# The self term of a graph layer's output: from a multiply-add on VectorE to a diagonal product on TensorE

## The reference

```python
def _gat_layer(x, src, dst, W, a_src, a_dst, b, heads, d_out, concat):
    h = (x @ W).reshape(N, heads, d_out)
    ...
    alpha = ex / (denom[dst] + 1e-16)
    msg = alpha[:, :, None] * h[src]
    out = jax.ops.segment_sum(msg, dst, num_segments=N)
    ...
loops = jnp.arange(N)
src = jnp.concatenate([edge_index[0], loops])
dst = jnp.concatenate([edge_index[1], loops])
...
x = x + gnn(_layernorm(x), ...)
x = x + ffn(_layernorm(x)[None], ...)[0]     # 768 -> 96 -> gelu -> 768
```

## Time and profile before

| | |
|---|---|
| median of three runs | 4394.83 us (4390.88 to 4399.89) |
| profiled execution | 4393.57 us, span 4391.8 us, mean granted clock of TensorE 0.911 |
| TensorE busy | 3519.7 us, 80% of the span |
| TensorE weight loads | 2144.6 us, 49% |
| VectorE busy | 2160.0 us, 49% |
| ScalarE, GpSimd | 30%, 25% |

### The profile page before, as it was taken

How to read it: one execution, slowest core, us unless ns; L and a number is a source line. 1 busy time by engine, 2 the same in 40 slices (tenths; PEclk the granted TensorE clock), 3 DMA queues, 4 the chain that set the end, 5 groups by cost and what they waited for, 6 DMA issues and landing times. The chain is left out here.

```text
span 4391.8 us, 67315 instructions
## 1 busy us (share of the span) xinstructions
PE 3519.7 (80%) x21804; PEld 2144.6 (49%) x21805; DVE 2160.0 (49%) x5207; ACT 1302.9 (30%) x2233; POOL 1088.3 (25%) x1396
## 2 busy tenths in 40 slices
PE   4850018999999999999999999999999900078988
PEld 3640005665556655565556655665556500055665
DVE  8877135334433444344433444344434200289998
ACT  3531104223332333223322333233322200034444
POOL 2447731000000000000000000000000067466665
PEclk9975559999999999999999999999999955589999
DMA  8862001111111111111111111111111000178887
GB/s 257 256 194 60 3 16 49 52 38 49 41 45 52 40 42 42 56 37 46 38 52 37 52 40 43 53 38 43 43 55 39 24 6 1 28 208 230 235 230 207
DMA packets 147719, 338.13 MB, mean 77 GB/s; under 512 B 81378, under 2 KB 82178, under 8 KB 140030
## 3 DMA queue, kind: packets, MB, share of 16 engines
q1 hardware_dynamic: 112047, 240.87, 18.1%
q0 software_dynamic: 34240, 93.39, 8.9%
q10 hardware_dynamic: 1175, 0.05, 0.0%
HBM read 266.08 MB, written 124.25 MB: 89 GB/s over the span
## 5 line engine op out<-in xcount | busy, mean ns | idle before, releaser
L934 POOL DMA_INDIRECT lay_rows<-parts,lay_idx x200 | 210.1, 1051 | 2533.1 <-PE lay_pz L1177 1615.8
L1211 PE MATMUL lay_pm<-lay_zh,w1h 128*128 128x500 f16 x1920 | 717.6, 374 | 26.5 <-DVE lay_h L1097 21.2
L1212 PE MATMUL lay_pm<-lay_zl,w1h 128*128 128x500 f16 x1920 | 717.9, 374 | 2.1 <-issue 1.7
L1213 PE MATMUL lay_pm<-lay_zh,w1l 128*128 128x500 f16 x1920 | 717.8, 374 | 0.0
L1018 DVE SCALAR_TENSOR_TENSOR lay_zl<-lay_pz,lay_zh 128x400 f16<-128x400 f32 x600 | 319.6, 574 | 708.5 <-ACT lay_zh L1128 708.5
L1128 ACT ACTIVATE lay_zh<-lay_pz 128x400 f16<-128x400 f32 x600 | 298.3, 504 | 1054.7 <-PE lay_pz L1177 1050.9
L1137 ACT ACTIVATE lay_ex<-lay_pm,b1c,scale 128x500 f32<-128x500 f32 x320 | 245.6, 768 | 869.5 <-PE lay_pm L1213 869.5
L1235 PE MATMUL lay_pm<-w2h,lay_gh 128*128 128x512 f16 x1280 | 484.9, 379 | 0.0
L1235 PE MATMUL lay_pm<-w2h,lay_gl 128*128 128x512 f16 x1280 | 483.9, 378 | 0.0
L1235 PE MATMUL lay_pm<-w2l,lay_gh 128*128 128x512 f16 x1280 | 483.4, 378 | 0.0
L1053 DVE TENSOR_SCALAR lay_ex<-lay_ex,scale 128x500 f32<-128x500 f32 x320 | 153.7, 480 | 568.2 <-ACT lay_ex L1137 568.2
(11 more groups left out here) (275 smaller groups left out, 5860.0 us busy)
## 6 DMA issues: line engine op xcount, KB each, us to landing
x<-in_x_dram SPq DMA_DIRECT2D x20, 1500.0 KB, 6.7
out_x<-x SPq DMA_DIRECT2D x100, 288.0 KB
out_own<-h SPq DMA_DIRECT2D x100, 288.0 KB
out_dram<-out_x SPq DMA_DIRECT2D x100, 288.0 KB
nrm_xb<-in_x_dram SPq DMA_DIRECT2D x20, 1344.0 KB
parts<-nrm_parts SPq DMA_DIRECT2D x20, 1344.0 KB
h<-lay_h SPq DMA_DIRECT2D x80, 336.0 KB
nrm_w<-in_L_gnn_W_dram SPq DMA_DIRECT2D x6, 1024.0 KB, 19.3
```

Source lines behind the costliest of these rows:

```text
L1211: pe.matmul(o, c.w1h[:, d, cols], zh[:, d, h], start=(d == 0), stop=False)
L1212: pe.matmul(o, c.w1h[:, d, cols], zl[:, d, h], start=False, stop=False)
L1213: ins = pe.matmul(o, c.w1l[:, d, cols], zh[:, d, h], start=False, stop=(d == DC - 1))
```

## The change

The self term moves from VectorE to TensorE. VectorE now writes for each tile a 100x100 diagonal matrix, `self_att`, the identity times the column of own weights, in the place where L1649 stood; it no longer reads `own` or `x` there. TensorE multiplies this diagonal by `own` and accumulates the product with that of `att` and `rows` in `pa`, in both column parts. The semaphore `own_added` is replaced: TensorE waits for `self_ready` and for the load of `own`, L1627 waits for the load of `x`, and SyncE frees a buffer of `own` by `agg_done`.

```diff
@@ stage_output, tiles
-        att = m.sb("att", [OE, AB, OT])
+        att, self_att = m.sb("att", [OE, AB, OT]), m.sb("self_att", [OT, AB, OT])
@@ SyncE, load_rows
-                    sp.wait_ge(own_added, t + 1 - HB)
+                    sp.wait_ge(agg_done, t + 1 - HB)
@@ VectorE, weights
-                    dve.wait_ge(own_added, GT * grp)
+                    dve.wait_ge(self_ready, GT * grp)
@@ VectorE, iteration
                     dve.wait_ge(agg_done, t + 1)
-                    dve.wait_ge(own_added, t + 1)
+                    dve.wait_ge(x_in[at], 32 * (grp + 1))
                     nc.vector.tensor_tensor(x[:, at], x[:, at], pa[0:OT, 0:D], ALU.add).then_inc(x2_ready, 1)
@@
                     spread(t2, at2)
-                    dve.wait_ge(x_in[at2], 32 * (there2 + 1))
-                    dve.wait_ge(own_in[at2 % HB], 32 * (2 * there2 + at2 // HB + 1))
-                    nc.vector.scalar_tensor_tensor(out=x[:, at2], in0=own[:, at2 % HB], scalar=w_own[:, at2:at2 + 1],
-                                                   in1=x[:, at2], op0=ALU.mult, op1=ALU.add).then_inc(own_added, 1)
+                    nc.vector.tensor_scalar(self_att[:, at2 % AB], c.ident[0:OT, 0:OT], w_own[:, at2:at2 + 1], None, ALU.mult)\
+                        .then_inc(self_ready, 1)
@@ TensorE, iteration
                     pe.wait_ge(gathered[at], 16 * (there + 1))
-                    pe.matmul(pa[0:OT, 0:512], att[:, at % AB], rows[:, at, 0:512], start=True, stop=True)
-                    pe.matmul(pa[0:OT, 512:D], att[:, at % AB], rows[:, at, 512:D], start=True, stop=True)\
-                        .then_inc(agg_done, 1)
+                    pe.wait_ge(self_ready, t + 1)
+                    pe.wait_ge(own_in[at % HB], 32 * (2 * there + at // HB + 1))
+                    for cols in (slice(0, 512), slice(512, D)):
+                        pe.matmul(pa[0:OT, cols], self_att[:, at % AB], own[:, at % HB, cols], start=True, stop=False)
+                        ins = pe.matmul(pa[0:OT, cols], att[:, at % AB], rows[:, at, cols], start=False, stop=True)
+                    ins.then_inc(agg_done, 1)
```

More of the change, by code:

```diff
@@ L1400, in stage_output @@
                 "turned", "xt_ready", "h_done", "u_ready", "t_ready", "th_ready", "g_ready", "o_done", "o_ready",
-                "own_added", "chain", "setup", "gelu", "prep", "bias_in", "held", "paused")
+                "self_ready", "chain", "setup", "gelu", "prep", "bias_in", "held", "paused")
         (par_in, turned_w, w_ready, init, posed, slots_in, idx_ready, mask_ready, looked, weights_ready,
          att_ready, agg_done, x2_ready, ve_ready, norm_ready, newton, xn_ready, turned, xt_ready, h_done, u_ready, t_ready,
-         th_ready, g_ready, o_done, o_ready, own_added, chain, setup, gelu, prep, bias_in, held, paused) = (
+         th_ready, g_ready, o_done, o_ready, self_ready, chain, setup, gelu, prep, bias_in, held, paused) = (
              m.sem(n) for n in sems)
```

## The result

The changed kernel takes 4429.77 us in the median of four runs (4427.81 to 4431.70), the one before 4392.87 in the runs beside it. The ratio is 1.0081 with a 95% interval of 1.0064 to 1.0099: 0.8% slower, as forecast. The profiled execution took 4428.32 us around a span of 4426.6.

The account below looks back on a forecast made before the run. VectorE bounds the kernel before, TensorE the changed one at 5.43 us per tile. Pace +32.1 and start +2.65 and +1.3 make +36 on 4393.6, about 4430 us; own range 4414 to 4445, stated range 4413 to 4452.

Parts of the forecast that it names:

- The bound and the room: In the loop, VectorE full at 4.79 us per tile, TensorE at 4.14, with 0.95 us of room there.
- The price of the product: TensorE's added 512- and 256-column f32 products take 1.29 us per tile, as the old aggregation and the projection do.
- The pace: Loop turns on TensorE of 5.43 us, 6.3 with look-ups; from tile 4 to tile 99, +32.1 us.
- The start: At tile 4: +2.65 us for its doubled aggregation, +1.3 for the transposes and first layer behind it.
- at the half clock: Tile 4's aggregation runs at 1.2 GHz, 2.65 us before the change, and doubles with the added product.
- The end of the span: Behind the last L1627 nothing changes: 19.7 us.
- VectorE's side at nothing: VectorE's tile loses 0.93 us (L1649), gains 0.27 (diagonal), to 4.13; this changes nothing if TensorE is the bound.
- The waits that go: In the loop, waits for gathered rows nearly gone, 10.3 us for own rows gone; lead grows 2 to 3 us.
- Rival A: TensorE has room: one record per product adds 0.645 us per tile, VectorE's relief counts, 4365 us; chance 0.04.
- B: Gathers stay late: a 1.0 us wait per group, then half clock, some 4 us per group, 4466 us; chance 0.11.
- C: TensorE's weight loads for the added products do not hide: 0.7 us per tile, 4496 us; chance 0.04.
- D: TensorE's added time comes near the room, 0.95 us per tile instead of 1.29: 4390 to 4400 us; chance 0.03.

## Why the prediction was right

**The bound and the room.** "VectorE full at 4.79, TensorE at 4.14 and 0.95 us of room per tile" was read from starts in the earlier trace rows. The run with the product on 512 columns, 0.86 us, comes out even; the changed kernel, 1.29, does not. That is the decisive step, and it is shown, though 0.95 itself is only bracketed by the two, and as a mean over the group it does not say what a single turn has: 0.65 in a plain one.

**The price of the product.** 1.29 us was taken from two neighbours of other heights. The trace after has 2.59 - 1.29 = 1.30, and the product issued twice adds it again.

**The pace.** 5.43 us per plain turn and 6.31 with look-ups were forecast as 5.43 and 6.3. From tile 4 to tile 99 the trace has 4406.65 - 3873.16 = 533.5 us against 531.9 computed; what is over are short delays before tile 5 of five groups (turns of 5.48 to 6.11), of which the trace names one as a wait for gathered rows.

**The start** was mis-sized: +3.95 us were reckoned and 3873.16 - 3872.28 = +0.9 came. The step that failed is "at the half clock" for tile 4: its aggregation took 2.64 us at full clock instead of 5.3 at half. The windows view from 3860 to 3870 us, of the kernel before, of the changed one, and of the one with both engines at work:

```profile
3860.00:3870.00 10.00, 5.32 (x23) 4.07 (x24) 5.90 (x18) 3.20 (x6) 7.34 (x17) 0.72 1.01 256
3860.00:3870.00 10.00, 4.77 (x31) 3.15 (x29) 6.34 (x23) 3.74 (x6) 5.55 (x16) 1.00 1.02 266
3860.00:3870.00 10.00, 5.25 (x17) 2.56 (x16) 5.71 (x18) 2.32 (x3) 7.48 (x17) 0.88 0.98 261
```

That the product itself, which keeps TensorE busier in the ten microseconds before (7.81 us against 4.88), raised the clock from 0.72 to 1.00 is near at hand but not shown: the kernel with both engines at work has the same 7.81 us and was granted 0.88, and the one with the product twice had 0.92 and fell to 0.74 in the ten microseconds after. The landing itself came 0.93 us later, 3870.32 against 3869.39. The end of the span, 19.95 us behind the last L1627, was 0.2 us longer than before. The sum of the span is +34.8 against +36.0 forecast: the start was 3 us too dear and the pace 1.6 us too cheap, two errors of opposite sign, and that part of the closeness is luck.

**VectorE's side at nothing.** Right, and shown by both engines doing the work. Its relief was sized at 0.66; the diagonal costs 0.18 us of path and not 0.27, so it is 0.75. It did not matter.

**The waits that go.** Gathers and own rows all but stopped being waited for, as argued from the lead. The prediction had the lead grow by 2 to 3 us to about 8, but the one gather that it showed had 7.8 already; over tiles 10 to 89 the lead went from 6.6 to 8.1 us in the median. SyncE waited 2.6 us in all for agg_done from 3900 to 4400 us, and neither that nor the added waits of TensorE's queue left a gap in TensorE's timeline.

**Rival A**, with the reading of TensorE's headroom by its weight loads, is refuted: they are busy 36.87 of 56.74 us, 65%, on an engine that has no gap left. What it asked for, one record per product, had its run, and there the record was also shorter: 0.34 us for both column parts, not the 0.645 of its arithmetic. By that arithmetic a group would take 41.4 + 3.4 + 1.8 = 46.6 us and the time would be some 4335; measured were 4373.69, with groups of 49 to 52 us. So the cheaper product did gain, but 38 us less than that, and the run without the product misses about as much (4330 expected, 4363 measured). That is the second limit, the loads, and the one thing the prediction did not see; its forecast did not need it, since a group of 56 us leaves the loads more time than the 48 to 53 of the run without the product.

**Rivals B, C and D** did not come: waits for rows are 0.4 us in total in the trace's list, the whole aggregation is 2.59 us from start to start, and the time is 37 us off the kernel before.

## What to carry to other kernels

Before moving work from the fullest engine to the next one, read both from start to start in one repeating turn: the move can pay only while the added time stays below the gap between the two sums, whatever the busy shares over the span say. Here the gap was 0.95 us in the mean of ten turns and 0.65 in a plain one; 0.86 broke even and 1.29 cost 37 us. Where the work alternates between engines, take the sums over the few turns that alternate, not over the group. A diagonal is a full matrix to TensorE, and in f32 it costs two records of every column; if the term can stand rounding, one record in a 16-bit type took about a quarter of the time (0.34 of 1.29 us). And when the bound is lifted, ask next how the loads arrive, not only what each engine adds up to.

## What the runs showed of the hardware

- Products of 512 f32 columns over 100, 97 and 128 partitions take the same 0.86 us from start to start, written or accumulated.
- A bfloat16 product of 512 columns took 0.23 us, 0.27 of the f32 one, with a moving operand that steps over every second element; 500 packed f16 columns took 0.21 us.
- Issuing DMAs whose addresses come from a table holds ScalarE about 1 us each (4.18 us for four), as it holds SyncE (3.95 us for four at 4019.46 in the kernel before); moved between queues, the cost moves with them. The record of the DMA instruction itself is some 0.35 us of each.
- In a stage's first 40 us, where TensorE still waits between its bursts, the granted clock differed between kernels with the same products on TensorE (1.00 and 0.88 from 3860 to 3870 us); a start priced at the half clock can come at the full one.
